# A four-stage convolution kernel: input in eight transfers on two queues, the pointwise convolution by pairs of quarters, and a part of the first stack copied by VectorE

## The reference

```python
x = x + L0(gn(x))   # the stage around the change
x = x + L1(gn(x))   # 3x3 convolution with bilinear taps
x = x + L2(gn(x))   # gated experts, two 3x3 convolutions, batch norms
x = x + L3(gn(x))   # mixed experts, two 3x3 convolutions
```

```python
para = relu(conv1x1(x, pw) + pb)            # 32 -> 16 channels
para = conv3x3(para, cw) + cb               # 16 -> 16
xu = patches(x, 3, 3)                       # 288 values per pixel
t = einsum('oje,bjp->boep', W, xu)          # 32 x 16 values per pixel
out = einsum('boep,bep->bop', t, para)
```

## Time and profile before

| | |
|---|---|
| median of 3 runs | 399.21 us (399.11 to 399.6) |
| the profiled execution, its own time | 398.11 us |
| its span | 395.9 us |
| mean granted TensorE clock | 0.986 |
| TensorE busy | 369.7 us (93%) |
| VectorE / GpSimd / ScalarE busy | 259.0 / 97.4 / 60.2 us |

### The profile page before, as it was taken

The page is one execution under the profiler, slowest core; times in us unless marked ns, Lnnn a source line. Parts: engine busy times, 40 slices in busy tenths (PEclk is TensorE's granted clock), DMA queues, the critical chain, the costliest instruction groups (busy, mean ns, idle before and its releaser), DMA issues.

```text
span 395.9 us, 8965 instructions
## 1 busy us (share of the span) xinstructions
PE 369.7 (93%) x3446; PEld 260.4 (66%) x3446; DVE 259.0 (65%) x465; ACT 60.2 (15%) x129; POOL 97.4 (25%) x248
## 2 busy tenths in 40 slices
PE   4699999999999999999999999899999979899991
PEld 4346888888888888888888888523367642466670
DVE  4643777887887878878878878724335196912255
ACT  1115110010010100100101000320031029442200
POOL 4332877888820000000000000106001019400000
PEclk9899999999999999999999999989999999999997
DMA  7542775716607538166184000198700000000022
GB/s 232 132 125 68 188 187 145 207 46 163 177 25 185 142 94 207 43 166 172 31 202 118 0 0 0 33 208 206 179 0 2 3 1 2 0 3 5 3 109 106
DMA packets 28320, 38.77 MB, mean 98 GB/s; under 512 B 7072, under 2 KB 23968, under 8 KB 27616
## 3 DMA queue, kind: packets, MB, share of 16 engines
q1 hardware_dynamic: 18336, 28.76, 28.1%
q10 hardware_dynamic: 9952, 9.56, 9.3%
HBM read 4.56 MB, written 2.10 MB: 17 GB/s over the span
## 4 chain that ended last, share of the span: by engine, by line
PE 87%; DVE 8%; issue 2%; POOL 1%; DMA 1%; SPq 1%; DVEq 0%; POOLq 0%
PE ps L858 23%; PE ps L859 22%; PE ps L860 8%; PE ps L907 7%; PE ps L1046 5%; PE ps L1030 5%; PE ps L891 4%; PE ps L975 2%; PE ps L999 2%; PE ps L833 2%; PE ps L1015 1%; PE ps L920 1%; PE ps L965 1%; DMA CWB<-in_cw 1%; PE ps L815 1%
## 5 line engine op out<-in xcount | busy, mean ns | idle before, releaser
L858 PE MATMUL ps<-WA,HS 128*128 128x512 f32 x384 | 153.6, 400 | 0.9 <-DVE TS L1104 0.9
L859 PE MATMUL ps<-WB,LS 128*128 128x512 f32 x384 | 150.8, 393 | 0.0
L1126 DVE TENSOR_TENSOR PROD<-ps,PT 128x512 f32<-128x512 f32 x128 | 88.4, 691 | 39.5 <-PE ps L860 33.1
L1110 DVE TENSOR_REDUCE RED<-PROD 128x32 f32<-128x512 f32 x128 | 86.4, 676 | 0.0
L858 PEld LDWEIGHTS ps<-WA,HS 128*128 128x128 f32 x384 | 72.4, 189 | 19.4 <-issue 1.1
L859 PEld LDWEIGHTS ps<-WB,LS 128*128 128x128 f32 x384 | 72.4, 189 | 15.0
L860 PE MATMUL ps<-WC,TS 96*128 96x512 f32 x128 | 50.7, 396 | 0.0
L476 POOL MEMSET IMG<- 128x67 f32 x1 | 0.2, 154 | 139.7 <-DVE X L1116 139.7
L716 ACT ACTIVATE HS<-HS 32x40 fp32r<-32x40 f32 x21 | 5.7, 274 | 164.4 <-DMA TS<-LO 164.0
L891 PE MATMUL ps<-REPL,ONE 128*128 128x256 f32 x120 | 28.0, 385 | 1.7 <-DVE X L1311 1.3
L907 PE MATMUL ps<-SK,WE 128*32 128x512 f32 x256 | 28.4, 602 | 0.0
(11 more groups left out here) (221 smaller groups left out, 334.1 us busy)
## 6 DMA issues: line engine op xcount, KB each, us to landing
LS<-HS SPq DMA_DIRECT2D x7, 960.0 KB, 5.7
HS<-HI SPq DMA_DIRECT2D x60, 80.0 KB, 2.4
SK<-IMG SPq DMA_DIRECT2D x32, 131.8 KB, 2.7
HS<-LO ACTq DMA_DIRECT2D x32, 80.0 KB, 2.6
LS<-LO ACTq DMA_DIRECT2D x32, 80.0 KB, 2.7
HS<-HI SPq DMA_DIRECT2D x30, 79.8 KB, 2.4
TS<-LO SPq DMA_DIRECT2D x36, 63.8 KB, 4.0
X<-in_x SPq DMA_DIRECT2D x4, 512.0 KB, 5.6
```

The costliest lines, as they stand in the source:

```text
L858: pe.matmul(ps[b][:, :], px(HS, dy), WA[:, dy, :], start=(dy == 0), stop=False)
L859: pe.matmul(ps[b][:, :], px(LS, dy), WB[:, dy, :], start=False, stop=False)
L1110: ve.tensor_reduce(RED[j % 2][:, 32 * b:32 * b + 32], PROD[b % 2][:, :].rearrange("p (o e) -> p o e", e=E0), AX.X, ALU.add).then_inc(sum_d ...
L1126: ve.tensor_tensor(PROD[b % 2][:, :].rearrange("p (o e) -> p o e", e=E0), ps[b][:, :].rearrange("p (o e) -> p o e", e=E0), para.broadcast_ ...
```

## The change

The input comes in eight transfers of 512 columns with a semaphore each; SyncE issues the even ones, ScalarE, ahead of all its other work, the odd ones. `rstd(1)` stands ahead of GpSimd's copies of `CWB`. The pointwise convolution takes quarters in pairs: a pair starts when five (then eight) normalized pieces are there, and issues each kind of matmul for all eight tiles before the next kind. The last image's part of `TS` in the first stack is copied by VectorE instead of by four transfers, between `LS` and `WB`. TensorE's first tile waits for three clears, and for the fourth only ahead of its matmul with `TS`.

```diff
+FIRST_REST = NREST - 5
-        x_in = [sem(f"x_in{i}") for i in range(4)]
+        x_in = [sem(f"x_in{k}") for k in range(NCH)]
+        def load_x(queue, k):
+            queue.dma_start(X[:, k * CH:(k + 1) * CH], x[:, k * CH:(k + 1) * CH]).then_inc(x_in[k], 16)
 @block.sync
-            for i in range(4):
-                sp.dma_start(X[:, i * 1024:(i + 1) * 1024], x[:, i * 1024:(i + 1) * 1024]).then_inc(x_in[i], 16)
+            for k in range(0, NCH, 2):
+                load_x(sp, k)
...
-            stack_third(sp, 0, 0, range(B))
+            stack_third(sp, 0, 0, (0, 1, 2))
 @block.gpsimd
+            rstd(1)
             gp.wait_ge(w_cw, 16 * 6)
             for g in range(1, 4):
                 gp.tensor_copy(CWB[32 * g:32 * g + 32, :, :], CWB[0:32, :, :]).then_inc(cw_copied, 1)
                 gp.wait_ge(cw_copied, g)
...
-            rstd(1)
 @block.scalar
+            for k in range(1, NCH, 2):
+                load_x(act, k)
...
-                    fix(half, it + 1, 16 * NREST * it + (16 * (NREST - 1) if half == 0 else 16 * NREST))
+                    fix(half, it + 1, 16 * NREST * it + (16 * FIRST_REST if half == 0 else 16 * NREST))
 @block.tensor
-            for j in range(4):
-                pe.wait_ge(norm0_done, min(2 * j + 3, NCH))
...
+            for pair in range(2):
+                pe.wait_ge(norm0_done, 5 if pair == 0 else NCH)
+                tiles = [(b, j) for j in (2 * pair, 2 * pair + 1) for b in range(B)]
+                for b, j in tiles:
+                    pe.matmul(ps[b][32 * j:32 * j + 32, :], PWB[32 * b:32 * b + 32, 0:32], even_odd_rows(b, 0, 8 * j, 8), start=True, stop=False)
+                for b, j in tiles:
+                    q0 = 1 if j == 0 else 0
+                    pe.matmul(ps[b][32 * j:32 * j + 32, q0 * W:CH], PWB[32 * b:32 * b + 32, 16:48], even_odd_rows(b, 1, 8 * j - 1 + q0, 8 - q0), start=False, stop=True)
+                for b, j in tiles:
+                    ins = pe.matmul(ps[4 + b][32 * j:32 * j + 32, 0:W], PWB[32 * b:32 * b + 32, 16:48], even_odd_rows(b, 1, 8 * j + 7, 1), start=True, stop=(j == 3))
+                for b, j in tiles:
+                    if j < 3:
+                        ins = pe.matmul(ps[4 + b][32 * j:32 * j + 32, 0:W], PWB[32 * b:32 * b + 32, 0:32], even_odd_rows(b, 0, 8 * j + 8, 1), start=False, stop=True)
...
-            def tile(half, t, b):
+            def tile(half, t, b, third_late=False):
...
+                if third_late:
+                    pe.wait_ge(first_fixed, 4)
                 pe.matmul(ps[b][:, :], px(TS, 0), WC[:, :], start=False, stop=True).then_inc(tile_done, 1)
...
-                        pe.wait_ge(first_fixed, 4)
+                        pe.wait_ge(first_fixed, 3)
...
-                        tile(half, t, b)
+                        tile(half, t, b, first and j == 0 and b == 0)
 @block.vector
-                if k % 2 == 0:
-                    ve.wait_ge(x_in[k // 2], 16)
+                ve.wait_ge(x_in[k], 16)
...
+            ve.wait_ge(lo_done, 3)
+            b, m = B - 1, SL // 2 - 1
+            for dy in (0, 2):
+                a = dy // 2 * W + 2
+                ve.tensor_copy(TS[0][32 * dy:32 * dy + 32, b, :, 0:m], LO[32 * b:32 * b + 32, :, a:a + m]).then_inc(first_third, 1)
+            for h in range(2):
+                ve.tensor_copy(TS[0][32:64, b, h, 0:m], LO[32 * b:32 * b + 32, 1 - h, h * W + 2:h * W + 2 + m]).then_inc(first_third, 1)
             ve.wait_ge(w0_split, 1)
...
-            ve.wait_ge(strip_rest[0], 16 * (NREST - 1))
+            ve.wait_ge(first_third, 4)
+            ve.wait_ge(strip_rest[0], 16 * FIRST_REST)
```

More of the change, by code:

```diff
@@ L239, in build @@
         first_fixed = sem("first_fixed")
+        first_third = sem("first_third")
         tile_done = sem("tile_done")
@@ L493, in _ @@
             step(gp.tensor_copy(PB8[0:112, :], PAR[0:112, PB:PB + 1]))
[L494 to L497, removed]
             def rstd(k):
@@ L504, in _ @@
             rstd(1)
+            gp.wait_ge(w_cw, 16 * 6)
+            for g in range(1, 4):
+                gp.tensor_copy(CWB[32 * g:32 * g + 32, :, :], CWB[0:32, :, :]).then_inc(cw_copied, 1)
+                gp.wait_ge(cw_copied, g)
             gp.wait_ge(norm0_done, NCH)
```

## The result

Over 17 runs each, the changed kernel has a median of 395.9 us (393.9 to 399.53), the kernel before 401.14 (396.46 to 407.42). The ratio is 0.9908, with a 95% interval of 0.9884 to 0.9933; it leaves out runs over 1.5% above the fastest of their kernel, which are 8 of the 17 before and none of the changed, so it understates the gain. Over all 74 runs of the kernel before and all 23 of the changed one (experiment 1 included) the means are 401.58 and 396.08: 5.5 us, with 1.1 either way from the two standard errors, 0.35 and 0.44. So it is faster, as forecast, but the absolute time lies 3.0 above the forecast 392.9 and 0.3 outside the range. Of these 3.0, 1.9 are the base: the three runs that I started from (399.21) were among the kernel's shorter ones (401.14 over 17). The other 1.1 are the gain, 5.2 between the medians instead of 6.3.

What follows compares the result with a forecast made beforehand. TensorE, busy at full clock from 63.2 to 247.95 us, was taken as the bound, so only an earlier first tile counts. Gains 0.2+2.0+3.9+0.18 = 6.3 us gave 392.9 us against the median 399.21; range 391.0 to 395.6.

Steps and rivals of the forecast that it cites:

- Part 1: Eight half-size input transfers from two engines: statistics end 0.2 us sooner; bounds 0.65 gained, 2.6 lost.
- Part 2: Deviation ahead of GpSimd's weight copies: power starts 2.0 us sooner; copies held up could end `LO` 1.3 later.
- Part 3: Pointwise convolution by pairs: 4.2 us instead of 9.05, net 3.9 gained, supposing no stretch at half clock.
- rival B: Pointwise tiles of two column groups don't overlap, so pairs bring nothing: 3.0 us lost, 395.9 us; chance 0.08.
- the sentence that takes the clock as staying up here: TensorE's gap ahead of the pointwise convolution shrinks from 3.0 to 1.8-2.7 us; clock stays up, otherwise 1.5 us lost.
- Rival A: The clock falls in the pointwise convolution all the same: 4.8 us gained, 394.4 us; chance 0.23.
- Part 4: VectorE's copies of the third stack's last batch ahead of `WB`: 1.4 us, hidden under 3.3 us of cover.
- Part 5: SyncE's twelve `TS` transfers land at 28.8, 1.7 us before the clear needs them; sixteen would lose 1.2.
- Part 6: TensorE's first tile starts behind the first of two last clears, the other hidden by six matmuls: 0.18 us gained.
- everything behind it moves along: At the main loop's first tile: whatever it starts earlier, 6.3 us, comes off the whole span.
- My own sign of being wrong: Wrong if the main loop isn't 210.8 us long, the clock is low elsewhere, or the first tile waits for a transfer.
- The case's own range: Whole kernel: 391.0 to 393.8 us, from the input's 0.65 or 0, 1.10 a pointwise step, 1.1 between profiled and timed.

Runs made afterwards that it cites:

- experiment 1: The changed kernel once more, no edit; median 396.01 us (391.93 to 399.74).
- experiment 2: The changed kernel with filler matmuls in TensorE's idle times behind the main loop; median 395.62 us (393.22 to 398.2).
- 5: The changed kernel with 8 of SyncE's 32 stack transfers behind the main loop issued by ScalarE; median 394.02 us.
- 6: The changed kernel with 8 stack transfers moved from SyncE to ScalarE and fillers in TensorE's idle times behind the main loop; median 393.25 us, ratio 0.9811 to the kernel before.
- 8: As 6, with one of ScalarE's six first stack transfers moved to SyncE (seven and five); median 393.91 us.
- 11: The changed kernel with all sixteen `TS` transfers by SyncE again and no copies of it by VectorE; one run, 404.31 us.
- 3: The kernel before with filler matmuls in TensorE's idle times behind the main loop; median 400.29 us (398.03 to 407.59).
- 7: The kernel before with split stack transfers and fillers behind the main loop; median 399.0 us, ratio 0.9984 to the kernel before.
- 12: As 6, with two more filler matmuls on the input ahead of the pointwise convolution; median 393.47 us, ratio 0.9794 to the kernel before.
- experiment 4: The changed kernel with the pointwise convolution by quarters again; median 397.48 us.

## Why the prediction was right in direction and wrong in size

**Part 1, the input:** 0.2 us, as taken. ScalarE's table load came behind its issues, not ahead of them. The rule that issuing engines share the same DMA engines (the Trainium skill, DMA: Bandwidth & Descriptors, section Issuing engines are not separate DMA queues) gave 0; the traces agree to within that 0.2.

**Part 2, the deviation:** 2.0 taken; the power starts 2.13 sooner in the profile (13.30 to 11.17), 0.2 of it the input's, and undoing this part costs 1.8. The feared delay of GpSimd didn't come: the copies took 1.42 us instead of 1.14 beside the normalization, and `LO` still began right behind it. The lock rule (the Trainium skill, SBUF — State Buffer, section SBUF: two separate sides) speaks of waiting to the end of the other engine's instruction. The trace agrees with it so read: the three copies lost 0.28 us together, beside a row of VectorE instructions that follow each other at 0.47 us. I had let the copies wait for the whole row.

**Part 3, the pairs:** 4.2 us reckoned, 4.38 or 4.39 measured in all five profiles with the clock up; eight tiles do overlap, and rival B is out. **One step that failed is the sentence that takes the clock as staying up here.** It held in the changed kernel's first profile, by chance: of the seven profiles that are alike up to this stage (changed, 1, 2, 5, 6, 8, 11) the clock fell in three (5, 6 and 8), and then the stage takes 5.96 to 6.02 us and the first tile starts near 32.6 instead of 31.0 to 31.5. Rival A, with 0.23, deserved nearly a half. I had taken the fillers' length from one profile and compared idle times alone. The size was near: 1.5 taken, 1.6 measured in the stage (5.99 against 4.38), 1.4 between the means of the first tiles (32.62, 31.24).

**Part 4, the copies:** 1.4 us taken, 1.4 measured, hidden. **Part 5:** the transfers didn't become the bound; without part 4 they would have, by more than I reckoned (2.3 against 1.2). **Part 6:** the first matmul starts 0.17 behind the clear of `TS` instead of 0.34: 0.17, as reckoned.

**The sum:** 6.3 at the first tile. In the first profile 5.58 came of it: 0.39 went to the slow issue, 0.18 to the length of the stage, the rest to small terms. The six profiles with the changed start have it at 31.52, 31.23, 30.98, 32.57, 32.68 and 32.61, mean 31.93; the kernel before (and experiments 3 and 7) at 37.10, 36.83 and 36.99, mean 36.97. Gained 5.0, the forecast case 5.5 to 6.0. The difference of the mean times, 5.5 with 1.1 either way, agrees with this.

**The step that cost more is in the frame of the sum:** "everything behind it moves along", with one profiled execution and three runs as the base. It makes 1.9 of the 3.0 us. The stages behind the main loop take a different time in each run, by whether the clock falls in their short idle times and by how such a stretch meets the stack transfers. Experiment 1 shows 2.7 us between two profiles of one program, and the kernel before ran from 396 to 407. I had seen the low stretch behind its main loop and left it out of the sum and of the range. My own sign of being wrong, "if the clock is low elsewhere", came true. The case's own range was loosely added too: its terms give 392.9-0.45-1.1 = 391.4 and 392.9+0.2+0.9 = 394.0, not 391.0 and 393.8. With the median of all 74 runs of before, 401.0, as base the forecast gain gives 394.7, inside the range; with 0.8 more for the clock (half of 1.6), 395.5, against 395.9 measured.

What isn't settled: why the clock falls in one run and not in the next at nearly the same idle time behind the loop. The experiments show that filled idle times went with a clock that held there (no low stretch between the loop and the expert stage in 6 and 12), but experiment 4 held it too without them, and the expert stage's own idle times weren't filled. The spread of 396 to 407 does go with the clock: in the 57 runs of the kernel before that have both on record the span goes from 394.2 to 405.3 us, but the span times the mean granted clock only from 388.1 to 393.3 (mean 390.6; the changed kernel's 23 runs: 383.1 to 389.2, mean 385.6). Which stretches these are in which run, only the profiles would tell.

## What to carry to other kernels

When a start is shortened, look at what TensorE does ahead of it and in the idle time that remains: whether the clock holds was worth 1.4 us here, as much as a small part of the edit, and one profile doesn't tell. Fillers of a fixed number last shorter or longer with the clock, and leave an idle time that differs from run to run. Find the transfer that will end last once the engine chain is shorter, as part 4 did, and measure what it would have cost. And take the base of a sum from many runs, with the later stages' own spread in the range: one profile's low stretches are not the kernel's.

## What the runs showed of the hardware

The low stretches in these profiles (the start among the fillers and the end aside) were from 3.4 to 10.2 us long. One of 3.4 cost up to 1.7 us, half its length (an estimate; measured 1.4 to 1.6 in the pointwise convolution); one that covered a wait which would have come otherwise cost less or nothing: the convolution behind the main loop took 31.0 and 30.3 us with one at its beginning, and 34.2 with the clock held up there, a wait of 3.3 us, and a low stretch behind it.

Thirty-two stack transfers of 132 KB took one queue 22 to 24 us to issue, about 0.7 each; with 8 of them on a second queue the first was done after 17 to 19. The wait ahead of the sixth part, with the clock up, was 2.8 to 3.9 us in five profiles with one queue and 1.2, 0.6, 0 and 0 in experiments 6, 7, 8 and 12 with two. The windows view of 260 to 266 us, experiment 2 (one queue) and 12 (two), shows what the second queue brought:

```profile
260.00:266.00 6.00, 6.00 (x60) 1.98 (x56) 3.08 (x5) 0.00 (x0) 6.00 (x3) 1.00 0.75 169
...
260.00:266.00 6.00, 6.00 (x60) 1.99 (x56) 3.08 (x5) 0.00 (x0) 6.00 (x3) 1.00 1.00 252
```

One queue left a quarter of the DMA engines' time unused (0.75, 169 GB/s); two filled it (1.00, 252 GB/s). By this view a third queue would find little left there; none was tried.

GpSimd's copies beside VectorE's normalization took 1.3 to 1.6 us instead of 1.14. And eight tiles of 32 x 32 in two column groups went through TensorE in the time of four in one: 4.38 us for the stage, where four quarters took 7.37 with the clock up (experiment 4).

The same 24 filler matmuls at the start lasted 6.93 to 8.42 us from one profile to the next, because the clock rose among them sooner or later.
